# Attention maxima by DMA into a free row of the turned queries, passes shifted by half a step, loops written out, 1/127 in PSUM

## The chip, the cores and the metric

One core of a Trainium2 chip (trn2) runs the whole program. The metric is device microseconds of one execution. TensorE is PE (matmuls; PEld are its weight loads), VectorE is DVE, ScalarE is ACT, GpSimd is POOL, SyncE is SP and only issues DMAs here.

## What is computed

Four gated residual blocks act on x (64 sequences of 128 tokens, 256 channels, fp32), with a context `ctx_1024` of the same shape:

```python
x = x + tanh(g_xattn[0]) * attention(layernorm(x), ctx, ctx)            # 16 heads of 16, softmax(q k / 4) v
x = x + tanh(g_ffn[0])   * bitnet(layernorm(x))                         # quantised w1, conv over 3 tokens, silu, quantised w2
x = x + tanh(g_xattn[1]) * attention(relu(n(x) Wq), relu(ctx Wk), relu(ctx Wv))
x = x + tanh(g_ffn[1])   * experts(layernorm(x))                        # 8 experts, 2 chosen of 2 groups, silu(g) * u, down
```

In `bitnet` each token's row is scaled by 127 / max(|row|), rounded, multiplied, and scaled back.

## The kernel before

x and the context stay in SBUF for the whole program, a tile is one sequence (128 tokens on 128 partitions), and there are 64 tiles. Four stages follow one another, with a barrier between: `attention_stage` with layer 0, `bitnet_stage`, `attention_stage` with layer 1 (after a small `projection_stage` that prepares weights), `expert_stage`. In each stage every engine runs a list of its own operations in an order written by hand, and semaphores (`reach(engine, semaphore, value)`) tie the lists together. The function `step(i, u)` holds what an engine does in step i for several tiles at once, each operation lagging behind tile i by a fixed number of steps (TL, SL, EL, VL, FL: 1, 2, 3, 4, 5 in layer 0, one more in layer 1). `run_steps` makes a hardware loop of `step` (eight steps written out in an attention loop, two groups in the others), `write_steps` writes all of them out. PE in attention is written out already.

**Attention.** Each head has 16 channels, split into high and low fp16 parts, in slots of 64 rows: of the four groups of 16 rows the fourth is spare (zero in q, 1 in its first row for k). Two heads lie over one another in the 128 rows, and a pair of matmuls on 64 rows each works on both halves. A tile passes these operations:
- ACT and POOL (layer 0) or PE, ACT and DVE (layer 1, with `turn_split`, `project`) make `q_stack` and `k_stack`; PE turns them (`turn_stack`, L556), DVE copies q (`q_turned`, L678), ACT copies k (`k_turned`, L745). Four buffers of each rotate.
- `do_scores(t, u, p)`, L509: scores with queries on partitions, in two passes p of eight heads, each into the same pair of PSUM banks `score`. DVE takes the maxima (`take_max`, L641), and scales and negates them to fp16 (`neg_max`, L693).
- `turn_maxima`, L497: PE turns them, DVE copies them (`neg_max_t`, L666).
- `do_scores_t(t, u, p)`: scores with keys on partitions, again in two passes, both into the same pair of banks `score_t`. L521 is the product, L526 a second product, against `spread`, that adds the negated maximum of each query. A pass starts when ACT has read the pass before it.
- ACT's `do_exp`, L716; PE's `do_values`, L541; ACT's eviction, L760; PE's `turn_out`, L551; DVE's `divide`, L651 and L654; POOL's addition to x, L796; DVE's `take_stats`, L646.

In layer 0 the step on PE is: scores pass 0, turn_maxima, scores_t pass 0, turn k, turn q, scores pass 1, scores_t pass 1, turn_out, values. ACT's is: exp pass 0, k_stack (L736), k_turned (L745), exp pass 1, q_stack (L751), eviction (L760). In layer 1 PE's step is: scores 0, turn_maxima, turn_split (L576), scores_t 0, turn_out, turn q, project q (L583), scores 1, scores_t 1, turn k, project k and v, values. There the one bank `turn` holds in turn the split, the q and the k transposes: turn q waits until DVE has copied `split_t` (L670, semaphore `s_copied`).

**Feed-forward (`bitnet_stage`).** 16 groups of 4 tiles, 8 chunks c of 128 hidden channels in each. Chunk c passes: PE (L868), ACT (L1046 the middle tap, L1049 `shifted` for the left tap), DVE (`convolve`, L937, the right tap), POOL (L1087), ACT's silu (L1029), PE's transposes (L890), DVE's maxima (`largest`, L952), POOL's scaling (L1094), DVE's rounding (L944). Per group DVE computes `token_scales` after chunk 2 (L960, L962, L965): on L962 it multiplies `peak_mid` by `level`, 1/127, a column in SBUF.

**Experts.** 16 groups, 8 experts each, three matmul products. Before its loop SP loads the raw weights in `load_experts`, called in layer 1's attention once POOL has made `cl_ok` reach 24, into the part of the context that is no longer needed.

## Time and profile before

| | us |
|---|---|
| runs: 1891.81, 1893.88, 1896.88 | median 1893.88 |
| profiled execution | 1889.21 |
| its span | 1887.5 |

| engine | busy us | share of the span |
|---|---|---|
| PE | 1598.1 | 85% |
| DVE | 1574.0 | 83% |
| ACT | 1186.2 | 63% |
| POOL | 865.3 | 46% |

The whole-span shares are averages over four stages. By the first and last instructions attention 0 runs from 48 to 378 us, feed-forward from 379 to 837, projection and attention 1 from 837 to 1305, the experts to the end. A busy share has to be read stage by stage. A row of the timeline has the start in us, the length in us, engine, line, operation, written tile <- read tiles, shapes, how many instructions it merges, and in brackets how long the engine had been idle before it and what ended that. Operations of one engine overlap a little: the next one's start less the own start is what an operation costs in a full row of them.

### The profile page before, as it was taken

The page shows a single profiled execution, that of the slowest core. Times are in us where ns is not written, and L with a number is a line of the kernel's source. Part 1 is how long each engine was busy: PE and PEld are TensorE (multiplying, and loading weights), DVE is VectorE, ACT ScalarE, POOL GpSimd, SP SyncE. Part 2 cuts the span into 40 slices and gives each one's busy share as a digit, 9 for nine tenths or more (in the row PEclk, how much of TensorE's full clock was granted, in tenths as well). Part 3 has the DMA queues.
Part 4 walks back from the last instruction along what each step waited for, and adds up shares of the span by engine and source line. Part 5 has one row for each costly group of instructions (what it writes and reads, how often), then busy time and mean ns, then how long its engine had stood idle before and what let it go on. Part 6 is the DMA issues. An engine that isn't in the chain of part 4 may idle for free. (4 is left out here: it accounts for less than half of the span.)

```text
span 1887.5 us, 52415 instructions
## 1 busy us (share of the span) xinstructions
PE 1598.1 (85%) x20058; PEld 1093.4 (58%) x20058; DVE 1574.0 (83%) x2977; ACT 1186.2 (63%) x1916; POOL 865.3 (46%) x932
## 2 busy tenths in 40 slices
PE   0799999846766676748999999996899999999998
PEld 0677777623444444435777777775465565655655
DVE  7799999858888889876888888886888888888885
ACT  1799989778777787716888888886233333323332
POOL 1455555427777777753333333332233333333332
PEclk9999999979999989969999999998899999999999
DMA  9200000000000000000002000000221211222212
GB/s 313 89 3 3 3 3 3 3 0 1 1 0 0 0 0 0 0 17 2 3 2 69 2 2 2 2 2 2 68 91 57 101 67 56 100 67 70 98 57 68
DMA packets 45470, 67.43 MB, mean 36 GB/s; under 512 B 6272, under 2 KB 36736, under 8 KB 45312
## 3 DMA queue, kind: packets, MB, share of 16 engines
q1 hardware_dynamic: 42944, 65.03, 10.4%
q8 instruction: 133, 2.18, 0.5%
q10 hardware_dynamic: 2368, 0.02, 0.1%
q14 instruction: 25, 0.20, 0.0%
HBM read 56.39 MB, written 8.65 MB: 34 GB/s over the span
## 5 line engine op out<-in xcount | busy, mean ns | idle before, releaser
L716 ACT ACTIVATE a_exp<-a_score_t 128x1024 f32<-128x1024 f32 x256 | 262.4, 1025 | 82.5 <-PE a_score_t L526 81.8
L641 DVE TENSOR_REDUCE a_maxes<-a_score 128x8 f32<-128x1024 f32 x256 | 311.0, 1215 | 0.5 <-PE a_score L509 0.5
L1539 POOL TENSOR_TENSOR e_a_parts<-e_act,e_a_parts 128x512 f16<-128x512 f32 x128 | 153.3, 1198 | 332.5 <-ACT e_a_parts L1510 332.5
L1510 ACT ACTIVATE e_a_parts<-e_act 128x512 f16<-128x512 f32 x128 | 80.6, 630 | 314.1 <-DVE e_act L1342 309.2
L1087 POOL TENSOR_TENSOR b_hidden<-b_hidden,b_shifted 128x508 f32<-128x508 f32 x128 | 161.7, 1263 | 124.4 <-DVE b_hidden L937 124.1
L1224 PE MATMUL e_up_ps<-e_n_turned,e_up_t 128*128 128x512 f16 x768 | 187.9, 381 | 9.7 <-DVE e_act L1338 9.7
L1238 PE MATMUL e_out<-e_down_t,e_a_parts 128*128 128x256 f16 x1536 | 188.5, 273 | 0.8 <-POOL e_a_parts L1539 0.8
L1224 PE MATMUL e_gate<-e_n_turned,e_gate_t 128*128 128x512 f16 x768 | 187.9, 381 | 0.2 <-issue 0.2
L1238 PEld LDWEIGHTS e_out<-e_down_t,e_a_parts 128*128 128x128 f16 x1536 | 149.6, 98 | 39.1 <-POOL e_a_parts L1539 1.1
L1094 POOL TENSOR_TENSOR b_hidden<-b_hidden,b_scales 128x512 f32<-128x512 f32 x128 | 168.2, 1318 | 2.9 <-ACT b_scales L1069 2.9
L774 POOL TENSOR_TENSOR a_split<-ctx,a_split 128x256 f16<-128x256 f16 (+1 forms) x64 | 42.9, 671 | 268.6 <-ACT a_split L733 268.6
L521 PE MATMUL a_score_t<-a_q_turned,a_k_turned 64*128 64x128 f16 x2048 | 144.2, 218 | 24.5 <-DVE a_neg_max_t L666 22.4
L868 PE MATMUL b_hid<-b_x_turned,w1t 128*128 128x512 f16 x512 | 140.3, 399 | 28.1 <-DVE b_hidden L937 24.8
L1333 DVE TENSOR_TENSOR e_act<-e_sig,e_gate 128x512 f32<-128x512 f32 x128 | 87.8, 686 | 77.3 <-ACT e_sig L1507 72.6
L526 PE MATMUL a_score_t<-a_neg_max_t,a_spread 64*128 64x128 f16 x2048 | 142.8, 217 | 0.0
L1224 PEld LDWEIGHTS e_up_ps<-e_n_turned,e_up_t 128*128 128x128 f16 x768 | 74.3, 98 | 104.9 <-DVE e_act L1338 16.6
L890 PE MATMUL b_peaks<-ident,b_hidden 128*128 128x128 f32 x512 | 85.7, 293 | 57.9 <-ACT b_hidden L1029 48.0
L745 ACT ACTIVATE a_k_turned<-a_turn 128x1024 f16<-128x1024 f16 x128 | 130.2, 1017 | 2.2 <-PE a_turn L556 2.2
L937 DVE SCALAR_TENSOR_TENSOR b_hidden<-b_hid,taps,b_hidden 128x508 f32<-128x508 f32 x128 | 94.8, 741 | 43.1 <-ACT b_shifted L1049 42.3
L890 PEld LDWEIGHTS b_peaks<-ident,b_hidden 128*128 128x128 f32 x512 | 61.6, 148 | 107.4 <-ACT b_hidden L1029 73.6
L521 PEld LDWEIGHTS a_score_t<-a_q_turned,a_k_turned 64*128 64x128 f16 x2048 | 96.4, 94 | 41.0 <-DVE a_neg_max_t L666 31.4
L1224 PEld LDWEIGHTS e_gate<-e_n_turned,e_gate_t 128*128 128x128 f16 x768 | 74.1, 98 | 64.3 <-issue 1.8
(206 smaller groups left out, 4041.7 us busy)
## 6 DMA issues: line engine op xcount, KB each, us to landing
ctx<-e_weights SPq DMA_DIRECT2D x64, 512.0 KB, 5.7
out<-x SPq DMA_DIRECT2D x16, 512.0 KB, 2.9
x<-in_x SPq DMA_DIRECT2D x3, 2048.0 KB, 19.0
ctx<-in_ctx SPq DMA_DIRECT2D x1, 4096.0 KB, 27.0
ctx<-in_ctx SPq DMA_DIRECT2D x1, 3072.0 KB, 16.5
a_exp<-in_L_ffn_w SPq DMA_DIRECT2D x2, 1024.0 KB, 9.7
x<-in_x SPq DMA_DIRECT2D x1, 1536.0 KB, 16.4
ctx<-in_ctx SPq DMA_DIRECT2D x1, 1024.0 KB, 13.4
```

The source lines that it names most:

```text
L521: nc.tensor.matmul(score_t[:, column(half, k)], k_turned[r:r + SLOT, u % 4, h // 2, :], q_turned[r:r + SLOT, u % 4, h // 2, :], start=True ...
L526: last = nc.tensor.matmul(score_t[:, column(half, k)], spread[r:r + SLOT, h // 2, :], neg_max_t[r:r + SLOT, u % 2, :], start=False, stop=True)
L641: nc.vector.tensor_reduce(maxes[:, p * PAIRS:(p + 1) * PAIRS], score[:, :].rearrange("p (h k) -> p h k", k=P), AX.X, ALU.max).then_inc(max ...
L716: nc.scalar.activation(exp32[:, u % 2, 2 * p:2 * p + 2, :], score_t[:, :].rearrange("p (g n) -> p g n", g=2), ACT.Exp, scale=DH ** -0.5 / ...
L745: nc.scalar.activation(k_turned[:, (u - TL) % 4, :, :], k_bank[:, :].rearrange("p (n k) -> p n k", k=P), ACT.Copy).then_inc(k_copied, 1)
L868: last = nc.tensor.matmul(hid[c % 2][:, :], w1t[:, d, c * P:(c + 1) * P], x_turned[:, u % 2, d, part, :, :].rearrange("p t k -> p (t k)"), ...
L890: last = nc.tensor.transpose(peaks[c % 2][:, k * P:(k + 1) * P], hidden[:, u % 2, c, k * P:(k + 1) * P], m.ident32[:, :])
L1087: nc.gpsimd.tensor_tensor(dst, dst, shifted[:, c % 2, :].rearrange("p (t k) -> p t k", k=P)[:, :, 0:P - 1], ALU.add).then_inc(conv_ok, 1)
L1094: nc.gpsimd.tensor_tensor(h, h, scales[:, (u - back) % 2, :], ALU.mult).then_inc(mult_ok, 1)
L1224: last = nc.tensor.matmul(dst[:, :], w[:, wpart, d, e * P:(e + 1) * P], n_turned[:, u % 2, d, part, :, :].rearrange("p t k -> p (t k)"), s ...
L1238: last = nc.tensor.matmul(dst, a_parts[:, e % 4, part, k * P:(k + 1) * P], down_t[:, wpart, e, :], start=(e == 0 and s == 0 and k % 2 == 0 ...
L1539: nc.gpsimd.tensor_tensor(a_parts[:, e % 4, 1, :], act3[:, e % 2, :], a_parts[:, e % 4, 0, :], ALU.subtract).then_inc(alo_ok, 1)
```

## The change

The maximum of each query no longer comes from a second product. PE turns the 16 columns of maxima, DVE copies them to `neg_max_t` (16 partitions), and SP moves them by two DMAs into the spare row 48 (and 112) of `q_turned`. The matching row of `k_turned` holds -1 (layer 0) or the squared scale (layer 1), so the first product subtracts the maximum. In layer 0 DVE's reduction writes the maxima straight to `neg_max`. Pass 1 of `do_scores_t` and its exponential run one step later than pass 0, and both have other places in the orders. DVE, ACT and POOL in layer 1, and all engines in feed-forward and experts, are written out. `load_experts` issues one piece per step from tile 32 on. 1/127 lies in the second column of the PSUM bank `magic`. `make_spread` and its tile are gone.

```diff
             @block.sync
             def _(sp):
+                def step(t, u):
+                    sp.wait_ge(m_copied, t + 1)
+                    for half in range(2):
+                        sp.dma_start(q_turned[half * SLOT + 3 * DH:half * SLOT + 3 * DH + 1, u % 4, :, :],
+                                     neg_max_t[half * PAIRS:(half + 1) * PAIRS, u % 2, :]).then_inc(max_in[half][u % 2], 16)
+                    if layer and t >= FIRST_PIECE:
+                        if t == FIRST_PIECE:
+                            sp.wait_ge(cl_ok, 3 * EXPERTS)
+                        load_experts(nc, sp, io, m, t - FIRST_PIECE)
+
+                write_steps(step, UNROLL, TILES, 0)
...
                 def turn_maxima(t, u):
-                    reach(pe, neg_ok, t + 1)
-                    nc.tensor.transpose(neg_turned, neg_max[:, u % 2, :, :].rearrange("p r n -> p (r n)"),
-                                        m.ident16[:, :]).then_inc(m_turn, 1)
+                    if layer:
+                        reach(pe, neg_ok, t + 1)
+                    else:
+                        reach(pe, max_ok, (t + 1) * 2)
+                    nc.tensor.transpose(neg_turned, neg_max[:, u % 2, :], m.ident16[:, :]).then_inc(m_turn, 1)
...
                 def do_scores_t(t, u, p):
                     if p == 0:
-                        reach(pe, m_copied, t + 1)
+                        for half in range(2):
+                            reach(pe, max_in[half][u % 2], 16 * (t // 2 + 1))
                     reach(pe, exp_ok, t * 2 + p)
                     for k in range(HG):
                         for half in range(2):
                             h, _ = head_of(2 * p + half, k)
                             r = SLOT * half
-                            nc.tensor.matmul(score_t[:, column(half, k)], k_turned[r:r + SLOT, u % 4, h // 2, :],
-                                             q_turned[r:r + SLOT, u % 4, h // 2, :], start=True, stop=False)
-                        for half in range(2):
-                            h, _ = head_of(2 * p + half, k)
-                            r = SLOT * half
-                            last = nc.tensor.matmul(score_t[:, column(half, k)], spread[r:r + SLOT, h // 2, :],
-                                                    neg_max_t[r:r + SLOT, u % 2, :], start=False, stop=True)
+                            last = nc.tensor.matmul(score_t[:, column(half, k)], k_turned[r:r + SLOT, u % 4, h // 2, :],
+                                                    q_turned[r:r + SLOT, u % 4, h // 2, :], start=True, stop=True)
...
                         turn_maxima(i - EL, uE)
+                    if run_second:
+                        do_scores_t(i - EL - 1, (uE - 1) % UNROLL, 1)
                     if run_project:
                         turn_split(i - 1, (u - 1) % UNROLL)
-                    if run_exps:
-                        do_scores_t(i - EL, uE, 0)
...
                     if run_scores:
                         do_scores(i - SL, uS, 1)
-                    if run_exps:
-                        do_scores_t(i - EL, uE, 1)
                     if run_turn and layer:
                         turn_k(i - TL, uT)
+                    if layer and run_exps:
+                        do_scores_t(i - EL, uE, 0)
...
                     if run_values:
                         do_values(i - VL, uV)
+                    if not layer and run_exps:
+                        do_scores_t(i - EL, uE, 0)
...
                 def step(i, u):
                     run_exps = inside(i - EL, TILES)
+                    run_second = inside(i - EL - 1, TILES)
...
-                    if run_exps:
-                        do_exp(i - EL, uE, 0)
+                    if run_second:
+                        do_exp(i - EL - 1, (uE - 1) % UNROLL, 1)
...
-                    if run_exps and layer:
-                        do_exp(i - EL, uE, 1)
                     if inside(i - TL, TILES):
                         reach(act, k_turn, i - (TL - 1))
                         nc.scalar.activation(k_turned[:, (u - TL) % 4, :, :], k_bank[:, :].rearrange("p (n k) -> p n k", k=P), ACT.Copy).then_inc(k_copied, 1)
-                    if run_exps and not layer:
-                        do_exp(i - EL, uE, 1)
+                    if run_exps and layer:
+                        do_exp(i - EL, uE, 0)
...
                         nc.scalar.activation(out_t_sb[:].rearrange("p n k -> p (n k)"), out_t[:, :], ACT.Copy).then_inc(evicted, 1)
+                    if run_exps and not layer:
+                        do_exp(i - EL, uE, 0)
...
-                run_steps(act, step, UNROLL, head, TILES, last_lag)
+                if layer:
+                    write_steps(step, UNROLL, TILES, last_lag)
+                else:
+                    run_steps(act, step, UNROLL, head, TILES, last_lag)
...
-                nc.vector.memset(level[:], 1.0 / 127.0).then_inc(level_ok, 1)
+                nc.vector.memset(magic[:, 1:2], 1.0 / 127.0).then_inc(level_ok, 1)
...
-                    nc.vector.scalar_tensor_tensor(out=peak_mid[:], in0=peak_mid[:], scalar=1e-5, in1=level[:, 0:1].broadcast_to([P, GT]),
+                    nc.vector.scalar_tensor_tensor(out=peak_mid[:], in0=peak_mid[:], scalar=1e-5, in1=magic[:, 1:2].broadcast_to([P, GT]),
...
+def load_experts(nc, sp, io, m, n):
+
+    if n < 2 * EXPERTS:
+        name = ("L1_ffn_gate_proj", "L1_ffn_up_proj")[n // EXPERTS]
+        sp.dma_start(m.expert_raw[n // EXPERTS][:, n % EXPERTS, :], io[name][n % EXPERTS]).then_inc(m.expert_loaded[n // EXPERTS], 16)
...
-                run_steps(dve, step, 2, head, GROUPS, lag, first=2)
+                write_steps(step, 2, GROUPS, lag, first=2)
```

## Rows read from the trace of the kernel before

**Rows 1.** Windows by stage: us, busy time (instructions) per engine, PEclk, DMA.
```profile
100.00:362.00 262.00, 243.75 (x5457) 193.94 (x5455) 244.39 (x486) 236.45 (x325) 147.51 (x216) 1.00 0.01 3
426.00:816.00 390.00, 268.46 (x1629) 171.23 (x1630) 339.26 (x627) 302.66 (x571) 300.04 (x237) 0.95 0.00 0
907.00:1280.00 373.00, 373.00 (x6622) 275.50 (x6621) 332.19 (x602) 311.95 (x492) 142.10 (x219) 1.00 0.04 11
1355.00:1860.00 505.00, 494.22 (x3562) 303.26 (x3561) 419.73 (x773) 156.33 (x265) 171.34 (x132) 1.00 0.23 79
```

**Rows 2.** Timeline of DVE, one row of a step in attention 0.
```profile
200.77 0.69 DVE L678 COPY a_q_turned<-a_turn 128x1024 f16<-128x1024 f16 x1 [0.25 <-PE a_turn L556]
```

**Rows 3.** Timeline of ACT, one step of attention 0.
```profile
194.94 1.02 ACT L716 ACTIVATE a_exp<-a_score_t 128x1024 f32<-128x1024 f32 x1 [0.45 <-PE a_score_t L526]
195.86 0.62 ACT L736 ACTIVATE a_k_stack<-ctx 128x512 f16 x1
...
198.19 0.64 ACT L751 ACTIVATE a_q_stack<-a_normed 128x512 f16<-128x512 f32 x1
198.71 0.61 ACT L760 ACTIVATE a_out_t_sb<-a_out_t 128x512 f32<-128x512 f32 x1
```

**Rows 4.** Timeline of PE, attention 1, from the split transposes to turn_q.
```profile
1100.37 0.61 PE L576 MATMUL a_turn<-ident,a_split 128*128 128x128 f16 x8
1100.91 0.23 PE L521 MATMUL a_score_t<-a_q_turned,a_k_turned 64*128 64x128 f16 x2
...
1101.46 0.66 PE L551 MATMUL a_out<-ident,a_out_t_sb 128*128 128x128 f32 x4
1101.96 0.44 PE L556 MATMUL a_turn<-ident,a_q_stack 128*128 128x128 f16 x5
```

**Rows 5.** Timeline of PE, one step of attention 0.
```profile
198.23 0.40 PE L509 MATMUL a_score<-a_k_turned,a_q_turned 64*128 64x128 f16 x8
198.56 0.23 PE L497 MATMUL a_turn<-ident,a_neg_max 128*128 128x128 f16 x1
...
199.66 0.62 PE L556 MATMUL a_turn<-ident,a_k_stack 128*128 128x128 f16 x8
200.12 0.61 PE L556 MATMUL a_turn<-ident,a_q_stack 128*128 128x128 f16 x8
200.66 0.40 PE L509 MATMUL a_score<-a_k_turned,a_q_turned 64*128 64x128 f16 x8
...
201.44 0.66 PE L551 MATMUL a_out<-ident,a_out_t_sb 128*128 128x128 f32 x4
202.02 1.08 PE L541 MATMUL a_out_t<-a_exp,a_v_pad 128*32 128x128 f32 x32
```

**Rows 6.** Timeline of ACT and PE in the drain of attention 0.
```profile
366.39 1.02 ACT L716 ACTIVATE a_exp<-a_score_t 128x1024 f32<-128x1024 f32 x1 [0.72 <-PE a_score_t L526]
368.01 0.60 ACT L760 ACTIVATE a_out_t_sb<-a_out_t 128x512 f32<-128x512 f32 x1 [0.60 <-PE a_out_t L541]
...
366.86 1.08 PE L541 MATMUL a_out_t<-a_exp,a_v_pad 128*32 128x128 f32 x32
```

**Rows 7.** Waits of SP's queue: waited for, us in total, times, longest.
```profile
SPq L1200 <- DMA e_weights<-e_w_rows: 17.5, 16, 1.2
```

**Rows 8.** Timeline of PE in the fill of attention 1.
```profile
875.63 0.61 PE L576 MATMUL a_turn<-ident,a_split 128*128 128x128 f16 x8
...
877.12 0.55 PE L556 MATMUL a_turn<-ident,a_q_stack 128*128 128x128 f16 x7 [0.32 <-DVE a_split_t L670]
```

**Rows 9.** Timeline of DVE, POOL and ACT in feed-forward, around L962.
```profile
610.70 1.18 DVE L962 SCALAR_TENSOR_TENSOR b_peak_mid<-b_peak_mid,b_level 128x4 f32<-128x4 f32 x1
...
612.03 0.75 DVE L937 SCALAR_TENSOR_TENSOR b_hidden<-b_hid,taps,b_hidden 128x508 f32<-128x508 f32 x1
...
610.59 1.27 POOL L1094 TENSOR_TENSOR b_hidden<-b_hidden,b_scales 128x512 f32<-128x512 f32 x1
...
610.84 0.67 ACT L1049 ACTIVATE b_shifted<-b_hid,taps 128x512 f32<-128x512 f32 x1
```

More of the change, by code:

```diff
@@ L408, in attention_stage @@
         q_copied, k_copied, m_copied = sem("q_copied"), sem("k_copied"), sem("m_copied")
+        max_in = [[sem(f"max_in{half}_{n}") for n in range(2)] for half in range(2)]
         scores_ok, max_ok, neg_ok = sem("scores_ok"), sem("max_ok"), sem("neg_ok")
@@ L703, in step @@
                         take_stats(i - STATS)
-                run_steps(dve, step, UNROLL, head, TILES, last_lag)
+                if layer:
+                    write_steps(step, UNROLL, TILES, last_lag)
+                else:
+                    run_steps(dve, step, UNROLL, head, TILES, last_lag)
             @block.scalar
@@ L764, in step @@
                                              scale=gate[:, 0:1]).then_inc(v_ok, 1)
-                run_steps(act, step, UNROLL, head, TILES, last_lag)
+                if layer:
+                    write_steps(step, UNROLL, TILES, last_lag)
+                else:
+                    run_steps(act, step, UNROLL, head, TILES, last_lag)
             @block.gpsimd
@@ L796, in step @@
                         nc.gpsimd.tensor_tensor(m.x[:, t, :], m.x[:, t, :], mixed[:, (u - FL) % 2, :], ALU.add).then_inc(fin_ok, 1)
-                run_steps(pool, step, UNROLL, head, TILES, last_lag)
+                if layer:
+                    write_steps(step, UNROLL, TILES, last_lag)
+                else:
+                    run_steps(pool, step, UNROLL, head, TILES, last_lag)
 def bitnet_stage(nc, io, m):
@@ L1074, in step @@
                                                  ACT.Copy).then_inc(hi_ok, 1)
-                run_steps(act, step, 2, head, GROUPS, lag)
+                write_steps(step, 2, GROUPS, lag)
             @block.gpsimd
@@ L1212, in step @@
                         spread_weights(s - 1, u - 1)
-                run_steps(sp, step, 2, head, GROUPS, lag, first=2)
+                write_steps(step, 2, GROUPS, lag, first=2)
                 sp.wait_ge(stored, 16 * GROUPS)
@@ L1323, in step @@
                             logits(s - 1, u - 1)
-                run_steps(pe, step, 2, head, GROUPS, lag, first=2)
+                write_steps(step, 2, GROUPS, lag, first=2)
             @block.vector
@@ L1463, in step @@
                             norm(s)
-                run_steps(dve, step, 2, head, GROUPS, lag, first=2)
+                write_steps(step, 2, GROUPS, lag, first=2)
             @block.scalar
@@ L1514, in step @@
                             split(s)
-                run_steps(act, step, 2, head, GROUPS, lag, first=2)
+                write_steps(step, 2, GROUPS, lag, first=2)
             @block.gpsimd
@@ L1542, in step @@
                             split_low(s)
-                run_steps(pool, step, 2, head, GROUPS, lag, first=2)
+                write_steps(step, 2, GROUPS, lag, first=2)
 def build_program(nc, io):
```

108 lines of the change are left out of this document (48 added, 60 removed).

## The prediction

> **What bounds the kernel now.** I read the busy times by stage first, then one step of each attention stage in the order of time, then the same places in the fill and the drain of the pipelines, where waits stand open that the steady state hides. The profiled execution took 1889.21 us (span 1887.5), the median of the three runs is 1893.88, so I add differences to the median.
>
> The stages have different limits [rows 1]. In attention 0 PE is busy 243.75 of 262 us, but DVE is what turns the step: its q_turned copy waits 0.25 us for PE's transposes in each step [rows 2], and PE in turn waited for DVE's maxima. ACT has 0.45 us left in each step [rows 3]: first exponential at 194.94, eviction at 198.71 lasting 0.61, then 0.45 of waiting, so a step is 4.83 us. In attention 1 PE is busy 373.00 of 373 us: it alone sets that step. In the feed-forward stage nobody is full, a chain through DVE, POOL and ACT sets the time. In the experts stage PE is busy 494.22 of 505 us.
>
> **Attention 0, part by part.** Out go, for each tile, sixteen matmuls against `spread`, DVE's scaling of the maxima, and PE's wait for the transposed maxima. Sixteen matmuls plus the change to other work take 0.55 us in a pass of `do_scores_t` (1100.91 to 1101.46) [rows 4], eight take 0.33 (198.23 to 198.56) [rows 5]; so a pass gets 0.22 shorter. With DVE as the limit this would be a gain. But the order moves too. In the new ACT order the first pass's exponential is the last thing of a step, and the second pass's is the first thing of the next one. Nothing lies between them. There is one pair of banks `score_t`: PE may write pass 1 only when ACT has read pass 0. Before, the k_stack and k_turned copies lay between and hid this turn-round; in the drain, where nothing lies between, it stands open: ACT idles 0.72 us between two exponentials (at 366.39) [rows 6]. Eight matmuls fewer make that 0.72 - 0.22 = 0.50.
>
> Count the new step from the start of the first exponential. The second starts at 1.02 + 0.50 = 1.52. Before, its successor on ACT started 0.92 after it; from first exponential to eviction ACT needed 198.71 - 194.94 = 3.77 [rows 3]. Now 3.77 - 0.92 + 1.52 = 4.37. The eviction also needs the values. PE starts pass 1 about 0.44 before the second exponential, at 1.08 (0.40 for eight matmuls, 0.04 to ACT). Then come +0.33 to turn_k, +0.46 to turn_q, +0.54 to the second scores, +0.33 to turn_out, +0.58 to the values [rows 5]: 3.32. The eviction starts 1.15 after the values do (366.86 to 368.01) [rows 6]: 4.47. The next first exponential follows 0.52 later (spacing of two such copies, 198.19 to 198.71 [rows 3]): **4.99 us** against 4.83. Pass 0 of the next tile is ready at 3.32 + 1.04 + 0.44 = 4.80 and doesn't delay it (1.04: 1.08 of values less the overlap). If PE's part were free, ACT alone would need 4.37 + 0.52 = 4.89. DVE, relieved by about 0.2 of scaling and by the 0.25 wait, would need some 4.4 and now waits for the others. So +0.16 for each of about 57 full steps: **+9.1 us**. Fill and drain: nothing, from -3 (shorter early passes) to +3 (half a step more at the end).
>
> **The DMA of the maxima.** SP now waits for `m_copied`, and issues two small transfers for each tile; behind that wait stand only SP's next transfers and the expert pieces. The trace of before has no copy from SBUF to SBUF. The nearest row is the experts' write of 16 KB: SP waits 17.5 us in 16 times for it, 1.09 each, behind an issue of about 0.3 [rows 7]; two in a row, some 2 us. From the end of the copy at about 0.7 in attention 0 there are 3.7 us until pass 0 at 4.36, in attention 1 about 3.5. So it is hidden; it decides from about 3.5 us on. Below nothing it cannot be. The Trainium skill's page "DMA: Bandwidth & Descriptors" (Anatomy of one DMA) gives about 2.0 us fixed for a transfer on another issue path; by that it stays hidden as well.
>
> **Attention 1.** PE is the limit, so its sum is the step. Two passes lose 0.22 each: -0.44. Pass 0 no longer shares an excursion with the second scores: it stands between turn_k and the projection. Each change between full matmuls and the 64-row ones costs 0.08 (0.54 against 0.46 after eight transposes [rows 5]); two more changes: +0.17. That leaves -0.27, if nobody waits. But one bank `turn` holds in turn the split, q and k transposes, and turn_q waits until DVE has copied the split ones. In the fill this wait stands open: split transposes at 875.63, turn_q at 877.12 after a wait for DVE [rows 8], 1.49 us apart at least. In the steady state they are 1.59 apart [rows 4]: 0.10 of slack, because pass 0 (0.55, and the change before it) lay between. The change takes the pass out of that gap and puts pass 1 ahead of the split. What remains between is 0.46 of transposes and 0.50 of turn_out [rows 4], 0.96. PE waits 1.49 - 0.96 = 0.53 in each step. Sum: -0.27 + 0.53 = **+0.26**, over about 60 steps with all parts **+15.6 us**, and +1 in the drain, where pass 1 now comes just ahead of its values. ACT isn't late: its eviction waits for the values now as before. DVE has 41 us idle in 373 [rows 1]. The expert pieces of 128 KB on SP stand behind a tile's maxima and have a step each to go; cost nothing, cover the step. Taken together the wait for the split copy takes the place of the matmuls removed.
>
> **Feed-forward.** With 1/127 in PSUM the operation on L962 has one input in SBUF. It takes 1.18 us for 4 columns and ends at 611.88, when POOL's L1094 (610.59 + 1.27 = 611.86) ends [rows 9]. So it is POOL that it waits for. Free of that, it takes some 0.2 and the convolution on L937 could start near 611.0; but that needs ACT's `shifted`, done at 610.84 + 0.67 = 611.51, so it starts about 611.55 in place of 612.03 [rows 9]. The next late thing is ACT. **-0.48** in 14 full groups: **-6.7 us**; bounds: 0 if ACT's other waits take it back, -14 if the whole 1.0 counts. The Trainium skill ("SBUF — State Buffer", Who interferes with whom) says that a VectorE instruction with two SBUF inputs contends with a GpSimd one that reads SBUF; the row agrees, and that page alone has no reason for less than the full second.
>
> **Loops written out.** In attention 1 and the experts PE, already full, hides any loop end on the other engines; taken at nothing, bounds -2 and +3 (more code to fetch). PE has gone through attention written out all the time, without a wait. `spread`'s making on POOL: nothing to -1. The Trainium skill ("Runtime: NRT & Kernel Launch", Instruction fetch mechanics) says a taken branch outside the window forces a fetch before going on; by it each loop removed would give something, and PE's busy share in rows 1 leaves it no place in those two stages.
>
> **Sum:** 9.1 + 15.6 + 1 - 6.7 = +19.0; 1893.9 + 19.0 = **1913 us**.
>
> **The rivals.**
> - *Both moves are harmless, the work removed counts.* Attention 0 would go to DVE's 4.4 (-0.43 x 57 = -25), attention 1 by -0.27 x 60 = -16, feed-forward -6.7: 1893.9 - 48 = 1846. For it: DVE is the limit today. Against it: one pair of banks `score_t`, one bank `turn`, and both waits open in the trace. If it holds in one attention stage only, 1870 to 1893.
> - *The terms cancel.* ACT's 4.89 in attention 0 (+3), 0.3 of wait in attention 1 (+2), -7 to -10 in feed-forward: 1889 to 1899.
> - *The clock.* In feed-forward, with PE busy 268.46 of 390 us, the granted clock is 0.95 [rows 1], against 1.00 in both attention windows. PE's idle time in attention 0 goes from 0.3 to about 1.1 us of 5, so stretches at 1.2 GHz may come there; PE has 3.4 us on the new chain, so one costs up to that. Five to seven such stretches: +15, 1928. The size is not shown by any row of attention.
> - *The transfers come late.* At 4.5 us each tile would wait 0.8 to 1.0 in both stages: +110, 2005. Rows 7 speak against it.
> - *The feed-forward edit does nothing* (PSUM doesn't free it): 1920, within the forecast.
>
> **How the numbers follow.** Forecast (1903 to 1923, ends from 4.89 to 5.03 in attention 0 and 0.4 to 0.6 of wait in attention 1): 0.63. Clock: 0.13. Late transfers: 0.04. Cancelling: 0.07. Faster in one or both attention stages: 0.13. The range must leave out no more than 2 in 10: it leaves the late transfers and the faster cases below, and goes from 1893 to 1932. A measurement can tell about 0.3% from no change, 1888 to 1900. Slower 0.80, same 0.08, faster 0.12.
>
> **What would show it.** Attention 0: first exponentials 4.99 apart, ACT idle 0.5 between the two of one tile, DVE idle over 0.4 in a step. Attention 1: steps of 7.1, PE waiting 0.5 for L670's copy ahead of turn_q, PE busy less than its whole window. L962 near 0.2, groups 0.5 shorter. PE's wait for `max_in` near nothing; over 0.1 in a step would make me wrong, as would attention steps under 4.83 and 6.81.

## The result and the profile after

The changed kernel took 1927.53 us (median of four runs, 1926.07 to 1932.86) against 1894.95 for the kernel before beside it: ratio 1.0179, 95% interval 1.0154 to 1.0203. The forecast was 1913, in a range of 1893 to 1932, and slower. Its profiled execution has a span of 1924.4 us against 1887.5, 36.9 more. The kernel before was timed again beside every experiment (medians 1891.38 to 1897.2), so kernels of different experiments are compared below by their ratios to it; one of the ten runs of experiment 1, of 3796.78 us, is left out of its ratio, and nothing here explains it. The stages of both traces are cut where ACT loads its table of functions anew:

| stage | before, us | after, us | difference | predicted |
|---|---|---|---|---|
| attention 0 | 331.0 | 335.8 | +4.8 | +9.1 |
| feed-forward | 458.2 | 448.5 | -9.7 | -6.7 |
| projection and attention 1 | 468.0 | 513.8 | +45.8 | +16.6 |
| experts | 582.2 | 578.4 | -3.8 | 0 |

The sign and the place were right, the size of attention 1 was not. The feed-forward stage and the experts gave back more than was forecast. Windows by stage, kernel after (us, busy time and instructions of PE, PEld, DVE, ACT, POOL, granted clock, DMA share, GB/s), to be held against [rows 1]:

```profile
100.00:362.00 262.00, 222.16 (x4496) 166.32 (x4496) 233.11 (x423) 235.81 (x318) 145.20 (x212) 1.00 0.01 3
400.00:820.00 420.00, 284.03 (x1750) 179.06 (x1748) 352.18 (x679) 329.01 (x622) 320.23 (x254) 0.98 0.00 1
900.00:1320.00 420.00, 374.93 (x5826) 252.45 (x5818) 305.68 (x609) 315.00 (x498) 145.14 (x220) 1.00 0.04 10
```

In attention 1 PE was busy in the whole window before; now it is busy 375 of 420 us, so it waits, 0.81 us in a step of 7.575. For what, PE's waits in 860 to 1340 us tell (waited for, us in total, times, longest):

```profile
PE a_turn L549 <- DVE a_split_t L670: 27.2, 61, 0.9
PE a_turn L549 <- DVE a_k_stack L682: 24.2, 63, 0.6
PE a_score_t L519 <- DMA a_q_turned<-a_neg_max_t: 2.4, 2, 1.4
```

The first wait is the one predicted. The second, in every step too, is not in the prediction. The DMA of the maxima is hidden but for two tiles, both at the end of the stage, where PE has little left to do between the copy and the pass (1334.22 to 1336.72, 2.50 us):

```profile
1334.01 0.21 DVE L666 COPY a_neg_max_t<-a_q_ps 16x128 f16<-16x128 f16 x1 [0.49 <-PE a_q_ps L495]
...
1336.72 0.40 PE L519 MATMUL a_score_t<-a_q_turned,a_k_turned 64*128 64x128 f16 x8 [1.44 <-DMA a_q_turned<-a_neg_max_t]
```

One step of PE, kernel after, attention 1 (start, duration):

```profile
1082.68 0.62 PE L569 MATMUL a_turn<-ident,a_split 128*128 128x128 f16 x8
1083.14 0.60 PE L544 MATMUL a_out<-ident,a_out_t_sb 128*128 128x128 f32 x4
1084.18 0.61 PE L549 MATMUL a_turn<-ident,a_q_stack 128*128 128x128 f16 x8 [0.43 <-DVE a_split_t L670]
...
1086.15 0.62 PE L549 MATMUL a_turn<-ident,a_k_stack 128*128 128x128 f16 x8 [0.38 <-DVE a_k_stack L682]
1086.70 0.40 PE L519 MATMUL a_score_t<-a_q_turned,a_k_turned 64*128 64x128 f16 x8
...
1088.43 1.08 PE L534 MATMUL a_out<-a_exp,a_v_pad 128*32 128x128 f32 x32
...
1089.93 0.40 PE L519 MATMUL a_score_t<-a_q_turned,a_k_turned 64*128 64x128 f16 x8
```

and DVE in the same step:

```profile
1083.34 0.69 DVE L670 COPY a_split_t<-a_turn 128x1024 f16<-128x1024 f16 x1 [0.67 <-PE a_turn L569]
1083.95 1.21 DVE L638 TENSOR_REDUCE a_maxes<-a_score 128x8 f32<-128x1024 f32 x1
1085.08 0.68 DVE L679 COPY a_q_turned<-a_turn 128x1024 f16<-128x1024 f16 x1
1085.68 0.41 DVE L682 SCALAR_TENSOR_TENSOR a_k_stack<-a_kv_ps,a_k_stack 128x256 f16<-128x256 f32 x1
```

The split transposes start at 1082.68; then DVE copies them, takes maxima, copies the turned queries and makes the low half of k, without a gap, and only then turn_k can start, at 1086.15: a chain of 3.47 us, which experiment 1 finds again in another order of PE. From turn_k to the next split transposes (1090.26) PE runs through in 4.11 us. 3.47 + 4.11 = 7.58 is the step. Before, the same chain ran beside PE's work: from the split transposes at 1100.37 [rows 4] turn_k followed after 3.56 us, behind work and not behind a wait, and 3.25 us later came the next split transposes; 6.81. In these rows of before, DVE's low half of k and then turn_k, PE doesn't wait:

```profile
1103.36 0.41 DVE L681 SCALAR_TENSOR_TENSOR a_k_stack<-a_kv_ps,a_k_stack 128x256 f16<-128x256 f32 x1
...
1103.93 0.62 PE L556 MATMUL a_turn<-ident,a_k_stack 128*128 128x128 f16 x8
```

So PE's time falls into a **covered part** (3.47 us, set by DVE) and an **open part**. Both passes lay in the covered part. The change moved them into the open one.

### The profile page after: what moved, and what is told of

It is laid out like the page before. It is cut to its first block and busy times, and to the rows that moved or that the text cites. A ratio compares the mean times of both kernels' runs of the same rounds, so it can differ in the third digit from the quotient of the medians.

```text
span 1924.4 us, 45924 instructions
## 1 busy us (share of the span) xinstructions
PE 1563.9 (81%) x18010; PEld 1030.6 (54%) x18010; DVE 1517.6 (79%) x2911; ACT 1189.1 (62%) x1916; POOL 862.6 (45%) x926
## 5 line engine op out<-in xcount | busy, mean ns | idle before, releaser
L783 POOL TENSOR_TENSOR a_split<-ctx,a_split 128x256 f16<-128x256 f32 x64 | 42.9, 671 | 318.4 <-ACT a_split L739 318.4
L879 PE MATMUL b_hid<-b_x_turned,w1t 128*128 128x512 f16 x512 | 135.2, 388 | 26.7 <-DVE b_hidden L948 23.5
L638 DVE TENSOR_REDUCE a_maxes<-a_score 128x8 f32<-128x1024 f32 x128 | 155.4, 1214 | 0.0
L641 DVE TENSOR_REDUCE a_neg_max<-a_score 128x8 f16<-128x1024 f32 x128 | 154.9, 1210 | 0.5 <-PE a_score L506 0.5
L519 PE MATMUL a_score_t<-a_q_turned,a_k_turned 64*128 64x128 f16 x2048 | 102.2, 219 | 47.3 <-ACT a_exp L721 43.7
L787 POOL TENSOR_TENSOR a_k_stack<-ctx,a_k_stack 128x256 f16<-128x256 f16 (+1 forms) x64 | 51.9, 810 | 166.3 <-ACT a_k_stack L742 166.3
L549 PE MATMUL a_turn<-ident,a_k_stack 128*128 128x128 f16 x1024 | 81.1, 223 | 50.2 <-POOL a_k_stack L787 25.6
L805 POOL TENSOR_TENSOR x<-x,a_mixed 128x256 f32<-128x256 f32 (+1 forms) x128 | 92.8, 725 | 55.6 <-DVE a_mixed L654 52.4
```

The source lines that it names most:

```text
L519: last = nc.tensor.matmul(score_t[:, column(half, k)], k_turned[r:r + SLOT, u % 4, h // 2, :], q_turned[r:r + SLOT, u % 4, h // 2, :], sta ...
L638: nc.vector.tensor_reduce(maxes[:, p * PAIRS:(p + 1) * PAIRS], score[:, :].rearrange("p (h k) -> p h k", k=P), AX.X, ALU.max).then_inc(max ...
L641: nc.vector.tensor_reduce(neg_max[:, u % 2, :].rearrange("p (r a k) -> p a r k", r=2, k=HG)[:, p, :, :], score[:, :].rearrange("p (r k n) ...
L879: last = nc.tensor.matmul(hid[c % 2][:, :], w1t[:, d, c * P:(c + 1) * P], x_turned[:, u % 2, d, part, :, :].rearrange("p t k -> p (t k)"), ...
```

## The experiments

**1. Both passes of attention 1 back into the covered part.** The changed kernel with

```
                     if run_project: turn_split(...)
+                    if run_second and layer: do_scores_t(i - EL - 1, ..., 1)    # was ahead of turn_split
...
+                    if layer and run_exps: do_scores_t(i - EL, uE, 0)           # was behind turn_k
                     if run_turn and layer: turn_k(i - TL, uT)
```

> The changed kernel, but on PE in attention 1 pass 1 of the transposed scores stands behind the split transposes (between them and turn_out), and pass 0 ahead of turn_k (behind the second scores), so both gaps that had cover before have it again. Everything else, the DMA and the shift by a step too, stays. Theory (the passes were moved out of the cover of DVE's chain): DVE's chain of 3.47 us from the split transposes to turn_k stays, then 0.45 + 1.39 + 1.01, with 0.40 ahead: step 6.72 us in place of 7.57, about 52 us less, 1875 us. Rival: the transfer of the maxima, 2.15 us from the end of DVE's copy to landing, has only 2.5 us here; if it doesn't fit, PE waits for it and the step stays over 7.0. Rival: second products removed are worth 0.44 only where PE has no waits at all: 7.1.

Measured: 1887.95 us, ratio to before 0.9978 (0.9967 to 0.9988), 2.0% below the changed kernel. Attention 1 took 469.3 us instead of 513.8, its step 6.81 us. PE, one step:

```profile
1105.57 0.22 PE L495 MATMUL a_q_ps<-ident,a_neg_max 128*16 128x128 f16 x1
1105.72 0.62 PE L569 MATMUL a_turn<-ident,a_split 128*128 128x128 f16 x8
1106.27 0.40 PE L519 MATMUL a_score_t<-a_q_turned,a_k_turned 64*128 64x128 f16 x8
...
1108.65 0.39 PE L519 MATMUL a_score_t<-a_q_turned,a_k_turned 64*128 64x128 f16 x8
1109.19 0.62 PE L549 MATMUL a_turn<-ident,a_k_stack 128*128 128x128 f16 x8 [0.15 <-DVE a_k_stack L684]
```

The wait ahead of turn_q is gone. The one ahead of turn_k stays, 0.15: from 1105.72 to 1109.19 it is 3.47 us again, the open part is now 3.34, and they add up to 6.81. The whole +45.8 us, but for 1.3, is the place of the two passes. The step is not the 6.72 us expected, and the time not 1875: the open part was taken as 3.25, as before, and it grew by 0.09. The split transposes come 0.15 us behind the transpose of the maxima in its new shape (1105.57 to 1105.72), and in the kernel before 0.06 us behind it, in this row and 1100.37 [rows 4]:

```profile
1100.31 0.23 PE L497 MATMUL a_q_ps<-ident,a_neg_max 128*128 128x128 f16 x1
```

The medians over the stage are 0.155 and 0.066. This also shows why the 0.44 us of matmuls removed are worth nothing here: they lay under DVE's chain and could give no more than its 0.10 of slack, and the new transpose takes that back.

**2. The low half of k off the chain.** The changed kernel, where DVE does L682 ahead of the split copy:

```
+                    if layer and inside(i - 2, TILES):      # ahead of the copy of the split rows, was behind q_turned
+                        reach(dve, v_ok, i - 1); nc.vector.scalar_tensor_tensor(out=k_stack[..., 1, :], ...)
```

> The changed kernel, but in attention 1 DVE makes the low part of k_stack (L682) ahead of the copy of the split transposes, in its idle time, in place of behind the maxima and the q copy. In the changed kernel an attention-1 step is 7.57 us, and PE waits 0.43 ahead of turn_q and 0.38 ahead of turn_k. Theory: one chain on DVE (split copy, maxima, q copy, k low part, 3.47 us from the split transposes to turn_k) sets the step; with the k low part out of it only the 1.49 us from the split transposes to turn_q are left: step 7.12 to 7.2, about 24 to 28 us less, 1900 to 1904 us. Rival: turn_q's wait alone sets the step (the blind prediction): the wait ahead of turn_k is only passed on and nothing changes, 1927 us. Rival 2: DVE as a whole is late (its queue grows by the earlier wait for ACT): no change or slower.

Measured: 1915.97 us, ratio 1.0135 (1.0112 to 1.0157). Attention 1 took 499.3 us, a step 7.32: 0.255 less, not 0.38. The wait for k's low half is gone, but turn_k now follows DVE's q_turned copy, the link before it in the chain:

```profile
1107.35 0.62 PE L569 MATMUL a_turn<-ident,a_split 128*128 128x128 f16 x8
...
1109.75 0.68 DVE L683 COPY a_q_turned<-a_turn 128x1024 f16<-128x1024 f16 x1
...
1110.57 0.61 PE L549 MATMUL a_turn<-ident,a_k_stack 128*128 128x128 f16 x8
```

The copy ends at 1110.43, and from the split transposes to turn_k it is 3.22 us, not 3.47. The chain was real, but only one link shorter; a third or more of the gain expected in a step (0.38 to 0.45) is missing for that reason.

**3. Passes earlier in attention 0.** The changed kernel, where pass 1 stands straight behind the first scores and pass 0 ahead of the values, and ACT does the exponential of pass 0 ahead of the eviction:

```
                     if run_scores: do_scores(i - SL, uS, 0)
+                    if run_second and not layer: do_scores_t(i - EL - 1, ..., 1)
                     if run_exps: turn_maxima(i - EL, uE)
...
+                    if not layer and run_exps: do_scores_t(i - EL, uE, 0)
                     if run_values: do_values(i - VL, uV)
```

> The changed kernel, but in attention 0 the first pass and its exponential stand one place earlier (PE: ahead of the values; ACT: ahead of the eviction), and PE's pass 1 straight behind the first scores. So ACT has the eviction between the two exponentials of a tile. Theory (ACT's turn-round between two adjacent exponentials sets the step, 0.5 us of idle in each): the turn-round is partly covered, step 4.5 to 4.6 in place of 4.96, 22 to 28 us less, 1900 to 1905 us. Rival: PE's chain or the transfer of the maxima (2.15 us to landing, window about 2.1 here) is as late: step 4.7 to 4.9, 4 to 16 us less. Rival: DVE has become the limit for another reason: no change.

A miss: 1940.55 us, ratio 1.0262 (1.0238 to 1.0287), some 15 us above the changed kernel (attention 0 took 350.5 us) instead of some 25 below. The step went from 4.96 to 5.18. ACT's turn-round is gone; two waits took its place, in every step. PE, then DVE:

```profile
205.51 0.40 PE L506 MATMUL a_score<-a_k_turned,a_q_turned 64*128 64x128 f16 x8 [0.43 <-DVE a_neg_max L643]
...
206.79 0.40 PE L519 MATMUL a_score_t<-a_q_turned,a_k_turned 64*128 64x128 f16 x8 [0.30 <-issue]
...
204.11 0.21 DVE L668 COPY a_neg_max_t<-a_turn 16x128 f16<-16x128 f16 x1 [0.47 <-PE a_turn L495]
204.25 1.20 DVE L643 TENSOR_REDUCE a_neg_max<-a_score 128x8 f16<-128x1024 f32 x1
```

Pass 1 ahead of turn_maxima makes DVE's copy late, the maxima behind it, and PE's next scores, which need the same banks. And pass 0 came too early for its transfer: DVE's copy ends at 204.32, pass 0 starts at 206.79, **2.47 us** later, behind 0.30 of waiting. The profile puts this wait down to "issue", nothing that it shows, in nearly every step, and names the transfer in two. But the last semaphore update of the transfer stands in the same trace: it comes 2.39 us after the copy's end (median), and pass 0 starts 0.09 us behind it, so the wait is for the transfer. That is the first price of the DMA seen from a copy to the matmul that needs it; the 2.15 us of the expectation were too few.

**4. ACT's exponentials apart.** The changed kernel, attention 0, with the k_stack copy between the two exponentials:

```
-                    if run_second: do_exp(i - EL - 1, ..., 1)
+                    if run_second and layer: do_exp(i - EL - 1, ..., 1)
                     ... k_stack copy ...
+                    if run_second and not layer: do_exp(i - EL - 1, ..., 1)
```

> The changed kernel with one edit in attention 0: ScalarE does the k_stack copy between the two exponentials of neighbouring passes, so that they are no longer adjacent. Theory (the step of 4.96 us is ScalarE's work plus one turn-round of 0.49 us in which it waits for the scores of pass 1, which TensorE can only write once the exponential of pass 0 has emptied the buffer): the copy of 0.52 us covers the turn-round, the step falls to between 4.5 and 4.8 us, whatever is late next (VectorE waits 0.40 us for the turned queries now), 64 steps give back 10 to 29 us, so 1899 to 1918 us against 1927.5. Rival (ScalarE's wait is only slack behind a cycle of TensorE and VectorE): the step stays at 4.96 and the time at 1927.

Measured: 1928.47 us, ratio 1.0178 (1.0157 to 1.0199), step 4.96: the rival held. ACT, then PE, one step:

```profile
197.83 0.60 ACT L766 ACTIVATE a_out_t_sb<-a_out_t 128x512 f32<-128x512 f32 x1 [0.28 <-PE a_out_t L534]
198.32 1.02 ACT L721 ACTIVATE a_exp<-a_score_t 128x1024 f32<-128x1024 f32 x1
199.23 0.63 ACT L742 ACTIVATE a_k_stack<-ctx 128x512 f16 x1
199.84 1.02 ACT L721 ACTIVATE a_exp<-a_score_t 128x1024 f32<-128x1024 f32 x1
...
194.44 0.40 PE L519 MATMUL a_score_t<-a_q_turned,a_k_turned 64*128 64x128 f16 x8 [0.68 <-ACT a_exp L721]
...
196.68 1.08 PE L534 MATMUL a_out_t<-a_exp,a_v_pad 128*32 128x128 f32 x32
197.70 0.40 PE L519 MATMUL a_score_t<-a_q_turned,a_k_turned 64*128 64x128 f16 x8
```

The copy does fill ACT's wait, but the step's circle doesn't pass through ACT's second exponential. It goes from pass 1 (194.44) through the turns, scores and values (196.68) to the eviction (197.83), the exponential of pass 0 (198.32) and back to pass 1 (199.40). This is the circle of the prediction's sum, term by term. What PE has to lose is the 0.68 us in which pass 1 stands for the exponential of pass 0.

**5. Low half of k ahead of the turned maxima.** Experiment 1, with L682 ahead of DVE's copy of the turned maxima and ACT's v_pad ahead of the eviction:

```
+                    reach(dve, v_ok, i - 1); nc.vector.scalar_tensor_tensor(out=k_stack[..., 1, :], ...)
                     ...
                     nc.vector.tensor_copy(neg_max_t[...], neg_turned)
```

> The kernel with the passes of attention 1 moved back beside VectorE's chain (labelled x2_l1_covered), and VectorE's low half of k moved off the chain between the split transposes and turn_k: it stands ahead of the copy of the turned maxima, in 0.67 us in which VectorE waits, and ScalarE writes v_pad ahead of the eviction so that it can. Theory (the step of 6.81 us there is VectorE's chain of 3.47 us and TensorE's 3.34 us from turn_k to the next split transposes): the chain loses the 0.33 us of the low half, the step is 6.48 to 6.55 us, and the time 1867 to 1871 us. Rival (TensorE or ScalarE by their own work hold the step at about 6.8): 1888 us, as that kernel.

Measured: 1894.1 us, ratio 0.9990 (0.9975 to 1.0005), step 6.88 instead of 6.48 to 6.55: a miss, and not the rival either, since PE doesn't fill the step by its own work: it waits 0.12 us ahead of pass 0 (median), in front of the transfer. DVE, then PE:

```profile
1103.82 0.42 DVE L668 SCALAR_TENSOR_TENSOR a_k_stack<-a_kv_ps,a_k_stack 128x256 f16<-128x256 f32 x1 [1.00 <-ACT a_v_pad L765]
1104.16 0.20 DVE L672 COPY a_neg_max_t<-a_q_ps 16x128 f16<-16x128 f16 x1
...
1106.86 0.40 PE L519 MATMUL a_score_t<-a_q_turned,a_k_turned 64*128 64x128 f16 x8
```

The copy of the maxima got late by the operation put ahead of it, and 1104.36 to 1106.86 is 2.50 us, the transfer again: it took the place of the wait for k.

**6. The order alone.** The kernel before with the new order of passes and exponentials, second products kept, no DMA.

> The kernel before with nothing but the new order of the passes and exponentials; the second products, their operand and the loops stay, and no DMA is added. Theory (the order alone costs the time, and the shorter passes give a part back): in attention 1 both passes, 0.55 us each with their second products, lie in the open stretch from turn_k to the next split transposes, so the step is about 3.47 + 3.25 + 2 x 0.55 = 7.8 us against 6.81; in attention 0 the turn-round of ScalarE is 0.49 us plus the 0.23 us of the second products, so 5.2 us against 4.83. Together 64 x 1.0 + 64 x 0.35 = 86 us: about 1977 us. Rival (the DMA, its queue or its semaphores cost the time, the order nothing): about 1891 us as before.

Measured: 1990.09 us, ratio 1.0496 (1.0475 to 1.0517). Steps 5.22 and 8.03; the second is 0.23 over the expectation, which had left out the changes between the two kinds of matmuls in the open part. So of the change's two halves in attention 1 the order costs 8.03 - 6.81 = 1.22 us a step, and the shorter passes give back 8.03 - 7.575 = 0.46; in attention 0 it is 0.39 against 0.26.

**7. The DMA without the order.** The changed kernel with the old order of passes and exponentials.

> The changed kernel with the order of the passes and exponentials of the kernel before: both passes of a tile in the step in which its maxima are turned; the DMA into the turned queries and everything else stays. Theory (what the shift by half a step buys is cover for the transfer: 2.5 us from the end of VectorE's copy to the pass, in x3_l0_covered and x9_l1_covered_klow_early): in attention 0 pass 0 began 0.05 us behind that copy, so the step grows by 2.4 us less the 0.4 us of the second products, to 6.8 us; in attention 1 pass 0 stands 0.6 us behind the copy and the step grows by 1.5 to 1.9 us, to 8.3 to 8.7 us; 64 x 2.0 + 64 x 1.7 = 237 us on 1880 us, 2080 to 2140 us. Rival (the transfer is fast and the shift was not needed): below the 1893 us of before, by the 0.42 us of TensorE's second products.

Measured: 2283.52 us, ratio 1.2055 (1.2032 to 1.2078), far more than expected. The mean steps are 7.6 us in attention 0 and 10.3 in attention 1, where 6.8 and at most 8.7 were expected. PE's waits for the transfer, in attention 0 and in attention 1:

```profile
PE a_score_t L519 <- DMA a_q_turned<-a_neg_max_t: 155.4, 57, 2.7
...
PE a_score_t L519 <- DMA a_q_turned<-a_neg_max_t: 135.9, 61, 2.8
```

One step of attention 0, PE and then DVE's copy:

```profile
207.84 0.60 PE L519 MATMUL a_score_t<-a_q_turned,a_k_turned 64*128 64x128 f16 x8 [2.73 <-DMA a_q_turned<-a_neg_max_t]
...
205.15 0.21 DVE L664 COPY a_neg_max_t<-a_turn 16x128 f16<-16x128 f16 x1 [1.42 <-PE a_turn L495]
```

and the window of attention 1:

```profile
900.00:1650.00 750.00, 564.68 (x6744) 396.45 (x6744) 441.07 (x859) 414.78 (x670) 242.88 (x313) 0.84 0.03 7
```

205.36 to 207.84 is 2.48 us, as in experiments 3 and 5, so the transfer has the price expected. What the expectation left out is the clock: PE idles over 2 us in a step, the granted clock falls to 0.89 in attention 0 and 0.84 in attention 1 (last row), and in many steps the eight matmuls behind the wait take 0.60 instead of 0.40. The shift by half a step is thus needed; it is its place that costs.

**8. The loops alone.** The kernel before with the later stages' loops written out.

> The kernel before with nothing but the loops of the later stages written out. Theory (VectorE's register arithmetic for the semaphore targets stood ahead of the work TensorE waits for in the experts): 16 groups of experts shorter by 0.35 us, less at the feed-forward, so 4 to 6 us less than before, 1885 to 1888 us. Rival (written-out code costs as much in instruction fetch as it saves, and the faster experts come from something else in the change): 1891 us, within 0.1% of before.

Measured: 1881.51 us, ratio 0.9929 (0.9911 to 0.9948), span 1879.5, 8 us less than the profiled execution of before (the rest of the 0.7% is not placed by the trace). Experts 578.3 us against 582.2, a group 34.11 instead of 34.45, as in the changed kernel; feed-forward 453.7 against 458.2, groups 26.11 instead of 26.26. The loss in attention 1 is not of the loops: with them written out the stage took 468.1 us, as before. In the loops of before the trace holds register operations on DVE for the semaphore targets (61 and 23 of two kinds in two groups of experts), written out there is none. The code has them ahead of what PE waits for, and these waits got shorter; the loops' branches went with them, and no run separates the two. PE's waits in experts, 1400 to 1850 us, before and then this kernel:

```profile
PE e_up_ps L1224 <- DVE e_act L1338: 9.1, 13, 0.7
PEld e_route_ps L1267 <- DVE e_weight L1392: 7.2, 13, 0.6
```

```profile
PE e_up_ps L1233 <- DVE e_act L1347: 7.3, 12, 0.6
PEld e_route_ps L1276 <- DVE e_weight L1401: 4.0, 13, 0.3
```

**9. 1/127 back in SBUF.** The changed kernel with a column `level` in SBUF instead of `magic[:, 1:2]`.

> The changed kernel with 1/127 back in a column of SBUF. Theory (the two SBUF inputs make L973, L962 before, wait for POOL): its mean goes from about 0.2 back to over 1.0 us, a feed-forward group from 25.70 to 26.2 us, 7 to 9 us more, 1935 us. Rival (the loops written out gave the feed-forward stage its 0.55 us a group): no change, 1927 us.

Measured: 1935.4 us, ratio 1.0233 (1.0211 to 1.0255), groups 26.09 us against 25.70. That is 0.39 in 14 groups, 5.5 us; the stage took 456.3 us against 448.5. The theory held in its mechanism (the operation's mean is over 1.0 us again). The rest of the 7.8 us, and so part of the agreement with 1935, goes with three groups of over 27 us where the changed kernel has one; experiment 10 takes them up.

**10. Loops and PSUM, attention untouched.** Experiment 8 with `magic[:, 1:2]`.

> The kernel before with the two parts of the change that don't touch the attention steps: the loops of the later stages written out, and 1/127 in PSUM. Theory (these are the gains, all of the loss is in attention): as labelled x7_written_out_only, with feed-forward groups of 25.70 us in place of 26.11, so 6 us less than that kernel in the span, 1873 to 1874 us; attention 0 and 1 keep their steps of 4.83 and 6.81 us. On the kernel before that is 13 to 20 us less, ratio 0.989 to 0.993. Rival (the groups got shorter in the changed kernel through something in attention or memory layout): groups stay at 26.1 us and the time is that of x7_written_out_only.

Measured: 1878.43 us, ratio 0.9929 (0.9911 to 0.9946), span 1879.2. L970 is short, groups are 25.71 us, yet the span is that of experiment 8: the 6 us expected did not come. Windows of two groups that follow each other:

```profile
609.86:635.58 25.72, 17.48 (x112) 11.21 (x112) 22.60 (x45) 21.01 (x41) 20.31 (x17) 1.00 0.00 1
635.58:662.65 27.07, 19.16 (x112) 12.15 (x112) 22.59 (x44) 21.11 (x41) 20.31 (x17) 0.94 0.00 1
```

The second group, in which the granted clock dips to 0.94, takes 1.35 us more. There are six such long groups of 14 here and one in the changed kernel; experiment 8 has two and the kernel before three, each 1.4 to 1.8 us longer than the usual group there. The dip alone doesn't make a group long: in the kernel before the group from 476.35 us took the usual 26.24 us at a mean clock of 0.93. So the edit's 0.40 us a group is sure, but what the stage gets of it depends on the number of such groups; between kernels with the same code in this stage it went from one to six. Why, stays open.

**11. A version that beats both.** The changed kernel; attention 0: pass 1 behind turn_q and ahead of the second scores, ACT as in experiment 4; attention 1: experiment 1, with L682 behind the copy of the maxima and ahead of the split copy, and v_pad ahead of the eviction.

```
                     turn_stack(q_bank, ...)
+                    if run_second and not layer: do_scores_t(i - EL - 1, ..., 1)
                     if run_scores: do_scores(i - SL, uS, 1)
```

> Attention 0: TensorE does pass 1 behind the turned queries and ahead of the second scores, ScalarE its exponential behind the k_stack copy. Attention 1: as labelled x2_l1_covered, with the low half of k behind the copy of the turned maxima and ahead of the copy of the split rows, and v_pad ahead of the eviction. Theory: the step of attention 0 is TensorE's stretch from pass 1 to pass 0 (3.26 us) and the 1.70 us in which pass 1 stands for the exponential of pass 0, of which TensorE waits 0.68; with 1.0 us of turns in that wait the step falls to 4.4 to 4.6 us, 64 x 0.4 = 26 us. In attention 1 pass 0 stands for the maxima, whose transfer takes 2.50 us from the end of VectorE's copy to the pass; begun 0.35 us earlier, the step of 6.88 of x9_l1_covered_klow_early falls to 6.6 to 6.7 us, 9 to 13 us below x2_l1_covered. Together about 1850 to 1862 us, ratio 0.976 to 0.984. Rival (in attention 0 the values, which need the exponential of pass 1, are late by as much as pass 1 was, so the wait only moves): the step stays at 4.9 and the time at about 1878 us.

Measured: 1852.42 us, ratio 0.9775 (0.9756 to 0.9795): 2.2% below before, 4% below the changed kernel. Attention 0 took 314.6 us, attention 1 459.6; steps 4.60 and 6.58 (median; mean 6.66). The time and the step of attention 0 lie in the ranges expected, the step of attention 1 at the edge of its own (6.6 to 6.7). PE and ACT in attention 0:

```profile
203.67 0.69 PE L549 MATMUL a_turn<-ident,a_q_stack 128*128 128x128 f16 x8
204.29 0.40 PE L519 MATMUL a_score_t<-a_q_turned,a_k_turned 64*128 64x128 f16 x8
...
202.94 1.02 ACT L723 ACTIVATE a_exp<-a_score_t 128x1024 f32<-128x1024 f32 x1 [0.27 <-PE a_score_t L519]
```

The turns now fill the time in which pass 1 waited for the exponential.

## Why the prediction was right and where it was wrong

**Attention 0, step of 4.99.** Measured 4.96, by the chain that was summed: pass 1 behind the exponential of pass 0, the values 3.31 after that exponential's start, the eviction 1.15 after these, the next exponential 0.49 later (experiment 4). The stage lost less than 9.1, +4.8, since the mean step of before was 4.85 (its loop ends) and not 4.83, and after 4.954: 0.10 x 57 = 5.8; the last 1.0 is not placed. The named place, ACT's idle time between the two exponentials, is there (0.49), but it was only a sign. Filling it changes nothing.

**Attention 1, +0.26 a step.** This step failed: measured +0.76. Right in it was the wait ahead of turn_q (0.43 shown, split transposes to turn_q 1.50 us against a forecast of 1.49). The error is in "PE is the limit, so its sum is the step": the working followed DVE's copy to turn_q and stopped there. Behind that copy DVE has maxima, q_turned and k's low half, and turn_k waits for the last, 3.47 us after the split transposes. So the -0.44 of shorter passes and their new place couldn't be added up as PE time: whatever left the covered part was lost (no gain), whatever entered the open part counted in full. That part went from 3.25 to 4.11 us, +0.86: 0.66 for the two passes, 0.10 for the change of work behind turn_k (0.55 to the next matmuls, 0.46 before), 0.09 for the transpose of the maxima (0.15 and 0.06). Less the 0.10 of slack that is +0.76. The trace of before shows it: DVE's low half of k ends at 1103.36 + 0.41 = 1103.77, turn_k starts at 1103.93; less the 0.06 from one to the other in the kernel after, 0.10 of slack. The size of +15.6 should have been about +45; experiment 1 shows it, and 6 from the other side.

**The time.** 1927.53 lies above the forecast's own band (1903 to 1923) and inside the range only because the range also covers the clock rival's 1928; the clock then stayed at 1.00 in both attention windows. So that the range held is in part luck: attention cost 50.6 us in the trace where 25.7 were summed, and feed-forward and experts gave back 13.5 where 6.7 were. The rival of cancelling terms adds up to 1889 to 1892 us, not to 1899.

**The DMA.** "Some 2 us" and hidden: 2.47 to 2.50 us from the copy's end to the pass (experiments 3, 5, 7), two issues of 0.63 us each among it, against windows of 3.7 us in attention 0 and 4.0 in attention 1 of the changed kernel (from 1082.67, where the copy ends, to 1086.70). Right, with less room in attention 0 than said.

**Feed-forward, -6.7.** L962 fell from 1082 to 158 ns (lines of DVE, kernel after):

```profile
L973 DVE SCALAR_TENSOR_TENSOR b_peak_mid<-b_peak_mid,b_magic 128x4 f32<-128x4 f32 x16 | 2.5, 158 | 0.6
```

and groups from 26.26 to 25.70, -0.56 against -0.48: 0.40 from PSUM (experiment 9), 0.15 from the loops. The rule of the Trainium skill quoted in the prediction ("SBUF — State Buffer", Who interferes with whom), two SBUF inputs against GpSimd, agrees with these numbers, 1082 ns with two inputs in SBUF and 158 with one. The other 2 us of the stage go with its long groups, one in place of three (experiment 10), and were not foreseen.

**Loops, 0.** Wrong by 3.8 us in the experts, and outside the bound of -2. PE was taken as full, which held for 494 of 505 us; in most of the remaining 11 it waits for DVE, and these waits got shorter when the loops were written out (experiment 8). By the Trainium skill's rule of taken branches ("Runtime: NRT & Kernel Launch", Instruction fetch mechanics), quoted in the prediction, each loop removed would give something, and something came; whether it came from the branches or from DVE's register operations no run tells.

**The clock.** In both attention windows it stayed at 1.00, with 0.8 us of idle PE in a step; at over 2 us idle it fell (experiment 7).

## What to carry to other kernels

Split the busy engine's step at the instruction that ends another engine's chain: work on one side is covered, on the other it counts in full, so a reordering is priced by what crosses that line, and follow the other engine's queue to its last consumer, not to the first. A wait that fills when you cover it proves nothing until the step gets shorter; look for the circle that returns to the same instruction one step later. A small transfer from SBUF to SBUF like this pair needs 2.5 us between producer and consumer, and every operation put ahead of its producer shortens that window.

## What the runs showed of the hardware

- Two transfers of eight rows of 256 bytes each within SBUF, issued one behind the other by SP: 2.47, 2.50 and 2.48 us from the end of DVE's copy to the matmul in three kernels (experiments 3, 5, 7). The last semaphore update comes 2.39 to 2.41 us after the copy's end (medians) in all kernels that have the transfers.
- Instruction blocks of 16 or 8 KB come as DMA transfers too, one every 7 us or so in attention 1 of the changed kernel; those of 16 KB take about 1 us each. In the changed kernel no block was under way during the transfers of 93 tiles, and none of these landed later than 2.6 us after the copy; for 35 tiles one was, and nine of them landed after 2.7 to 3.9 us. Over the nine kernels with the transfers it is 0 of 815 tiles against 79 of 337. So the blocks go with the late transfers in every case; that they are the cause was not tested by moving them. The late ones cost little: in the changed kernel three tiles of attention 0 waited 0.13 to 0.24 us, in experiment 11, with less room, five tiles of attention 1 waited 0.25 to 1.38 us.
- PE idle for over 2 us in each step of 7 to 10 (experiment 7) took the granted clock to 0.89 and 0.84 on average, the latter being a third of the time at 1.2 GHz instead of 2.4. In attention 1 PE waited 136 us for transfers, and the stage got 223 us longer than before.
- Changes of shape on PE cost some 0.09 us each here: from the start of eight transposes to the next matmuls it is 0.46 us when these are full ones and 0.55 when they have 64 rows; from the transpose of the maxima to the split transposes it is 0.066 us with 128 columns and 0.155 with 16 (medians; before, the changed kernel and experiment 1).
